# Weight slabs of the QKV and gate projections by casting GpSimd DMAs into one buffer, and other prefetches moved, in an attention and feed-forward layer on eight cores

## The chip, the cores and the metric

The kernel runs on all 8 cores of one Trainium2 chip. No core talks to another: each computes 2048 of the 16384 tokens, with 1536 tokens of history (the halo) in front of them. The metric is the device time of the slowest core, in microseconds.

## What is computed

```python
x = L0_attn_x                                   # (2, 8192, 1024)
xn = layernorm(x)
x = x + attn(xn) + ffn(xn)

def attn(x):                                    # 16 heads of 64, 44 fixed offsets up to 1536
    xn = scale * x / rms(x)
    q, k, v = split(xn @ w_qkv)
    scores[n, o] = q[n] . k[n - offset[o]] / 8 + pos_bias[o]
    out = softmax(scores) weighted sum of v[n - offset[o]]
    gate = sigmoid(xn @ w_gate + b_gate)
    x = x + (out * gate) @ w_out
    xn2 = rmsnorm(x)
    return x + (silu(xn2 @ w_ffn_gate) * (xn2 @ w_ffn_up)) @ w_ffn_down      # 2816 wide

def ffn(x):                                     # 4096 wide, ternary weights with a scale per row
    h = silu(x @ w1 * s1) * (x @ w2 * s2)
    h = gelu(h @ h1 * sh1); h = gelu(h @ h2 * sh2)
    return h @ w3 * s3
```

All tensors come in as f32; the matrix products are made in bf16 with f32 sums.

## The kernel before

The program is written as one list of instructions per engine. Each instruction waits for counters (`tM` counts matmul groups, `vC` VectorE instructions, `sC` ScalarE instructions, one more counter for each DMA stream). VectorE waits for its own previous instruction each time. `DA` puts a DMA on SyncE's (SP's) queue, `DSC` on ScalarE's, `DW` on GpSimd's (POOL's); only the last kind casts f32 to bf16 on the way. Every queue and engine takes its list strictly in order, so a DMA whose wait isn't fulfilled holds all that stand behind it. `barrier()` makes each engine wait for everything issued so far. Five stages follow one another, with a barrier after each.

- **Stage 0, norms (L263 to L423).** Before it, the mask table is written 16 times 512 KB to `d_grep` by 16 DMAs on SP. Then 7 blocks of 512 tokens. For block b: `p0_load(b)` (L325) loads x twice, as f32 into `s_x32` (L329, ScalarE's queue, 2048 KB) and as bf16 into `s_xb` (L333, POOL, 1024 KB written), each with two buffers. `p0_stats` (L338) squares on VectorE (L342) and sums both on TensorE by a column of ones. `p0_rows` (L358) is a chain of small one-partition instructions on VectorE and ScalarE, ending in three broadcasts by TensorE (L382 to L385). `p0_apply` (L389) is 24 VectorE instructions, which leave the normalised block in `s_xnb` and the scaled one in `s_xa`; then a store of `s_xnb` to `d_xn` (L406, on POOL, behind which the next `s_xb` load stands). The order in loop turn b is: load(b+1), rows(b), stats(b+1), apply(b).
- In turns 0 and 1 there is in addition `p1_slab` (L280), which fetches a weight slab for the K projection: twice, an SP DMA of half a slab in f32 (1024 KB) into the single buffer `s_w832` (L284), and a VectorE cast of it into one of two bf16 buffers `s_w8` (L288).
- **Stage 1, projections (L437 to L532).** Eight slabs of 1024 x 512 weights: two for K (448 matmuls together), two for Q (128 each), two for the gate (128 each), two for V (224 each). All but the K slabs call `p1_slab` at their beginning. Its second SP DMA waits for the first cast, and both casts stand in VectorE's list behind the evacuations of the slab before. K and V are kept on chip, Q and the gate go to DRAM through one buffer `s_evq`, so that there each evacuation waits for the store before it.
- **Stage 2, attention (L556 to L764).** The masks come back by 48 SP DMAs (L559), then 16 query tiles of 128 tokens. `p2_tile_loads` (L596) loads the next tile's q and gate on SP in the first head of a tile; pass A (L607) for that tile needs q one head later. At a tile's end the gated rows are stored (L754, SP).
- **Stage 3, output projection and second norm (L766 to L913).** After the barrier POOL issues 144 small loads of scales (L796 to L802); the first `s_xn2` instruction (L905) waits for all of them. `w_out` comes in two f32 halves on ScalarE's queue into one buffer, each followed by a VectorE cast (L810, L815), ahead of all other VectorE work. The gated rows come back in blocks of 4 tiles into two buffers (L828), each block loaded one ahead.
- **Stages 4 and 5**, the two feed-forward nets (L920 to L1143), take their weights by casting POOL DMAs.

## Time and profile before

| what | value |
|---|---|
| runs of the kernel | 4970.8 and 5433.37 us, median 5202.08 |
| the profiled execution | 4969.86 us |
| span on its slowest core (core 7) | 4968.3 us |
| spans of the eight cores | 4939.0 to 4968.3 us |
| granted TensorE clock, mean, core 7 | 0.847 |
| TensorE busy | 3896.4 us, 78% |
| VectorE busy | 1044.5 us, 21% |
| ScalarE busy | 663.1 us, 13% |
| POOL busy | 284.4 us, 6% |
| largest piece of the chain that ended last | matmuls of L1075 (stage 5), 47% |

The profile shows one execution on its slowest core; times are from the first to the last instruction of that core, and some 1.6 us of the execution lie outside of this span. The profiled execution is as long as the shorter of the two runs, so parts of the span can be set directly against 4970 us, and not against the median.

### The profile page before, as it was taken

Reading aid. Unit: us, or ns where it says so; the run is one execution under the profiler, and the core shown is the slowest. Engines: PE = TensorE matmul, PEld = TensorE weight load, DVE = VectorE, ACT = ScalarE, POOL = GpSimd, SP = SyncE. Lnnn points to the kernel's source line nnn. Section 1 sums busy time; section 2 is a strip of 40 time slices with the busy share of each in tenths; the row PEclk is TensorE's granted clock in tenths of the full one; section 3 lists DMA queues with packets and bytes.
Section 4 is the critical chain, followed back from the end, with each engine's and each line's share of the span. In section 5 each row is a group of like instructions: output and inputs, shape, how many; then the busy total and the mean of one; then the engine's idle time right before and its main releaser. Section 6 shows DMA issues by size and latency. Waiting matters only on the chain.

```text
span 4968.3 us, 53354 instructions; the slowest of 8 cores (4939.0 to 4968.3 us)
## 1 busy us (share of the span) xinstructions
PE 3896.4 (78%) x19714; PEld 1847.9 (37%) x19714; DVE 1044.5 (21%) x2055; ACT 663.1 (13%) x802; POOL 284.4 (6%) x310
## 2 busy tenths in 40 slices
PE   1126657455555456998898999999989899999999
PEld 0002223344444212443343444444434344444444
DVE  1564224454555332031011000000010200000001
ACT  0000010344444201200110000000002000000000
POOL 0000000000000510000010000000001000000000
PEclk8557888555555567999999999999999999999999
DMA  5340221100000223205466565656575656565657
GB/s 132 93 102 26 76 76 31 29 20 19 16 21 15 72 78 75 44 1 123 106 76 90 68 85 68 82 71 82 80 152 73 89 70 83 70 83 68 85 68 144
DMA packets 482017, 353.38 MB, mean 71 GB/s; under 512 B 41555, under 2 KB 438868, under 8 KB 479716
## 3 DMA queue, kind: packets, MB, share of 16 engines
q0 software_dynamic: 396064, 216.62, 33.2%
q1 hardware_dynamic: 77364, 114.46, 7.7%
q10 hardware_dynamic: 8336, 18.87, 1.2%
q8 instruction: 164, 2.69, 0.2%
q14 instruction: 89, 0.73, 0.1%
HBM read 513.43 MB, written 53.54 MB: 114 GB/s over the span
## 4 chain that ended last, share of the span: by engine, by line
PE 68%; DVE 12%; DMA 11%; issue 4%; POOL 2%; ACT 1%; DVEq 1%; SPq 1%; another core or an unknown queue 0%; ACTq 0%; POOLq 0%
PE p L1075 47%; DVE s_at L693 4%; PE p_f L950 3%; PE p_f L1009 3%; PE p_f L974 3%; PE p_B L668 3%; PE p_gm L455 2%; PE p_gm L515 2%; DMA s_xb<-xT 2%; PE p_av L715 1%; DMA s_w<-wqkv 1%; DVE s_b L629 1%; DMA d_gate<-s_evq 1%; DMA s_hs<-h1T 1%; PE p_o L869 1%
## 5 line engine op out<-in xcount | busy, mean ns | idle before, releaser
L1075 PE MATMUL p<-s_hb,s_hs 128*128 128x512 bf16 x6144 | 1335.3, 380 | 51.1 <-DMA s_hs<-w1T 24.4
L1075 PE MATMUL p<-s_ha,s_hs 128*128 128x512 bf16 x5120 | 1111.7, 381 | 45.7 <-DMA s_hs<-h1T 37.3
L1075 PEld LDWEIGHTS p<-s_hb,s_hs 128*128 128x128 bf16 x6144 | 598.1, 98 | 788.3 <-issue 76.7
L1075 PEld LDWEIGHTS p<-s_ha,s_hs 128*128 128x128 bf16 x5120 | 500.9, 98 | 656.6 <-issue 55.9
L1133 DVE SCALAR_TENSOR_TENSOR s_oo<-p,s_s,s_rr 128x1024 f32<-128x1024 f32 x16 | 20.5, 1284 | 2005.5 <-PE p L1075 1920.9
L715 PE MATMUL p_av<-s_V,s_at 128*128 128x65 bf16 x2048 | 193.7, 236 | 279.8 <-DVE s_at L693 277.8
L679 ACT ACTIVATE s_E<-p_B,s_negB 128x512 bf16<-128x512 f32 x512 | 351.7, 687 | 421.1 <-PE p_B L668 336.5
L715 PEld LDWEIGHTS p_av<-s_V,s_at 128*128 128x128 bf16 x2048 | 125.3, 118 | 371.9 <-issue 371.6
L668 PE MATMUL p_B<-s_qt,s_K 64*128 64x128 bf16 x2048 | 254.1, 308 | 0.0
L693 DVE TENSOR_TENSOR s_at<-s_E,s_MT 128x512 bf16<-128x512 bf16 x512 | 217.8, 425 | 171.6 <-DVE s_at L693 59.2
L668 PEld LDWEIGHTS p_B<-s_qt,s_K 64*128 64x128 bf16 x2048 | 197.7, 138 | 28.6
L455 PE MATMUL p_gm<-s_xa,s_w 128*128 128x512 bf16 x704 | 158.5, 389 | 53.2 <-DVE s_w L288 27.3
L382 PE MATMUL p_b<-s_row,s_onesf 1*128 1x512 f32 x14 | 14.3, 1122 | 225.2 <-DVE s_row L380 225.2
L1113 ACT ACTIVATE s_ha<-p,s_sh 128x1024 bf16<-128x1024 f32 x64 | 71.2, 1113 | 815.8 <-PE p L1075 815.8
L1113 ACT ACTIVATE s_hb<-p,s_sh 128x1024 bf16<-128x1024 f32 x64 | 71.3, 1113 | 784.9 <-PE p L1075 784.8
L950 PE MATMUL p_f<-s_xn,s_wga 128*128 128x512 bf16 x704 | 154.7, 384 | 20.3 <-DMA s_wga<-wfg 20.3
L1102 DVE SCALAR_TENSOR_TENSOR s_ha<-p,s_s,s_ha 128x1024 bf16<-128x1024 f32 x64 | 82.2, 1284 | 414.7 <-PE p L1075 414.7
L1009 PE MATMUL p_f<-s_hatt,s_wd 128*128 128x512 bf16 x704 | 153.6, 382 | 17.3 <-DMA s_wd<-wfd 17.3
L974 PE MATMUL p_f<-s_xn,s_wga 128*128 128x512 bf16 x704 | 152.1, 379 | 2.2 <-ACT s_hatt L959 2.2
L1096 ACT ACTIVATE s_ha<-p,s_s 128x1024 bf16<-128x1024 f32 x64 | 71.3, 1113 | 502.0 <-PE p L1075 502.0
L515 PE MATMUL p_gm<-s_w,s_xa 128*128 128x512 bf16 x448 | 102.4, 393 | 28.8 <-DVE s_w L288 28.6
L455 PEld LDWEIGHTS p_gm<-s_xa,s_w 128*128 128x128 bf16 x704 | 69.8, 100 | 143.0 <-issue 65.7
(108 smaller groups left out, 1758.8 us busy)
## 6 DMA issues: line engine op xcount, KB each, us to landing
s_hs<-h1T POOLq DMA_DIRECT2D x32, 2048.0 KB, 18.4
s_hs<-h2T POOLq DMA_DIRECT2D x32, 2048.0 KB, 16.1
s_hs<-w1T POOLq DMA_DIRECT2D x32, 512.0 KB, 5.9
s_hs<-w2T POOLq DMA_DIRECT2D x32, 512.0 KB, 5.9
s_hs<-w3T POOLq DMA_DIRECT2D x8, 2048.0 KB, 18.6
s_x<-xT ACTq DMA_DIRECT2D x7, 2048.0 KB, 17.9
s_w<-wqkv SPq DMA_DIRECT2D x12, 1024.0 KB, 5.2
d_grep<-d_gtab SPq DMA_DIRECT2D x16, 512.0 KB, 44.5
```

Source lines behind the costliest of these rows:

```text
L455: T(lambda t, oc4=oc4, kc=kc, b0=b0, b=b, p=p, w83=w83: t.matmul(p[:, b * 512:(b + 1) * 512], w83[:, kc, oc4 * 128:(oc4 + 1) * 128], xa3[: ...
L515: T(lambda t, tt=tt, kc=kc, p=p, w83=w83: t.matmul(p[:, 0:512], xa3[:, kc, tt * 128:(tt + 1) * 128], w83[:, kc, :], start=(kc == 0), stop= ...
L668: T(lambda t, jj=jj, ktile=ktile, g=g, r0=r0, pB=pB, q3=q3: t.matmul(pB[:, jj * 128:(jj + 1) * 128], K3[r0:r0 + 64, g, ktile * 128:(ktile ...
L679: SE(lambda s, pB=pB, par=par, hx=hx, bi=bi: s.activation(s_E[par][:, hx * HW2:(hx + 1) * HW2], pB[:, hx * HW2:(hx + 1) * HW2], AF.Exp, bi ...
L693: V(lambda v, h=h, par=par, hx=hx: v.tensor_tensor(s_at[par][:, hx * HW2:(hx + 1) * HW2], s_E[par][:, hx * HW2:(hx + 1) * HW2], MT3[:, h, ...
L715: T(lambda t, jj=jj, ktile=ktile, h=h, pav=pav: t.matmul(pav[:, 0:65], s_at[par][:, jj * 128:(jj + 1) * 128], V4[:, ktile, h, :], start=(j ...
L950: T(lambda t, oc=oc, kc=kc, b=b, pf=pf: t.matmul(pf[:, b * 512:(b + 1) * 512], wga3[:, kc, oc * 128:(oc + 1) * 128], xn23[:, kc, b * 512:( ...
L974: T(lambda t, oc=oc, kc=kc, b=b, pf=pf: t.matmul(pf[:, b * 512:(b + 1) * 512], wga3[:, kc, oc * 128:(oc + 1) * 128], xn23[:, kc, b * 512:( ...
L1009: T(lambda t, oc=oc, kc=kc, b=b, pf=pf: t.matmul(pf[:, b * 512:(b + 1) * 512], wd3[:, kc, oc * 128:(oc + 1) * 128], ha3[:, kc, b * 512:(b ...
L1075: T(lambda t, o2=o2, kc=kc, b=b, pp=pp, src3=src3, sl3=sl3, n_kc=n_kc: t.matmul(pp[:, b * 512:(b + 1) * 512], sl3[:, kc, o2 * 128:(o2 + 1) ...
L1102: V(lambda v, oc=oc, pp=pp: v.scalar_tensor_tensor(h53[:, oc, :], pp[:, :], s_s2[:, oc:oc + 1], h53[:, oc, :], ALU.mult, ALU.mult), waits= ...
L1113: SE(lambda s, oc=oc, pp=pp: s.activation(dst3[:, oc, :], pp[:, :], AF.Gelu, scale=ssc[:, oc:oc + 1]), waits=[(tM, fm)])
```

## The change

- Stage 0: the f32 load of x and the store to `d_xn` both go to SP's queue. POOL has only the `s_xb` loads left. The two K slabs aren't fetched here any more.
- Stage 1: there is one bf16 slab buffer. Each of the eight slabs is fetched whole by one casting POOL DMA (1024 KB written, 2048 KB read), which waits for the last matmul of the slab before. No cast on VectorE is left.
- Stage 2: the first half of `w_out` comes by a casting POOL DMA at the stage's beginning, and the first block of gated rows by an SP DMA at the end of query tile 3.
- Stage 3: only the second half of `w_out` is fetched in f32 and cast. The gated rows have one buffer, and the load for blocks 1 to 3 waits for the last matmul of the block before.

```diff
-    def p1_slab(src_slab):
-        si = p1w["idx"] & 1
-        p1w["idx"] += 1
-        for hf in range(2):
-            DA(qWS, lambda s, src_slab=src_slab, hf=hf: s.dma_start(
-                w8323[:, :, :], src_slab[:, hf * 4:(hf + 1) * 4, :]),
-               waits=[(vC, p1w["cast_prev"])])
-            wq = qWS.n
-            V(lambda v, si=si, hf=hf: v.tensor_copy(
-                s_w8[si][:, hf * 2048:(hf + 1) * 2048], s_w832[:, :]),
-              waits=[(qWS, wq)] + ([(tM, p1w["mms_done"][si])] if hf == 0 else []))
-            p1w["cast_prev"] = vC.n
-        return si, vC.n
...
-        DSC(qX0[p], lambda s, cslice=cslice, p=p: s.dma_start(
+        DA(qX0[p], lambda s, cslice=cslice, p=p: s.dma_start(
             s_x32[p][:, :].rearrange("p (c t) -> p c t", c=8), xTv[:, :, cslice]),
...
-        DW(qXN[p], lambda s, cslice=cslice, p=p: s.dma_start(
+        DA(qXN[p], lambda s, cslice=cslice, p=p: s.dma_start(
             xn_w[:, :, cslice], s_xnb[p][:, :].rearrange("p (c t) -> p c t", c=8)),
            waits=[(vC, apl_ms)])
...
-        if blk <= 1:
-            k_pre.append(p1_slab(wqkv_v[:, :, D + blk * 512: D + (blk + 1) * 512]))
...
-            if not is_q:
-                si, cast_v = k_pre[wh]
-            else:
-                si, cast_v = p1_slab(wqkv_v[:, :, base_col + wh * 512: base_col + (wh + 1) * 512])
-            w83 = w83v[si]
+            DW(wSL, lambda g, base_col=base_col, wh=wh: g.dma_start(
+                w83[:, :, :], wqkv_v[:, :, base_col + wh * 512: base_col + (wh + 1) * 512]),
+               waits=[(tM, tM.n)])
+            wslabq = wSL.n
...
-        si, cast_v = p1_slab(wgate_v[:, :, wh * 512:(wh + 1) * 512])
-        w83 = w83v[si]
+        DW(wSL, lambda g, wh=wh: g.dma_start(
+            w83[:, :, :], wgate_v[:, :, wh * 512:(wh + 1) * 512]),
+           waits=[(tM, tM.n)])
...
+    DW(qWO, lambda g: g.dma_start(
+        wo3a[:, :, :], wout.ap().rearrange("(k p) o -> p k o", p=128)[:, 0:4, :]))
+    p3_pre = {"g4q0": 0, "woq": qWO.n}
     p2_tile_loads(0)
...
+        if qt == 3:
+            DA(qG4, lambda s: s.dma_start(
+                g43[:, :, :], d_gated.ap().rearrange("n p d -> p n d")[:, 0:4, :]),
+               waits=[(qGD[0], st_p2["gd_store"][0]), (qGD[1], st_p2["gd_store"][1])])
...
-    for wh in range(2):
-        DSC(qWOB, lambda s, wh=wh: s.dma_start(
...
+    DSC(qWOB, lambda s: s.dma_start(
+        s_wo_b32[:, :].rearrange("p (k o) -> p k o", k=4),
+        wout.ap().rearrange("(k p) o -> p k o", p=128)[:, 4:8, :]),
+        waits=[(tM, tM.n)])
+    wob_q = qWOB.n
+    V(lambda v: v.tensor_copy(s_wo_b[:, :], s_wo_b32[:, :]), waits=[(qWOB, wob_q)])
...
-    g4_load(0, [(tM, tM.n), (vC, p2_end_v)])
-    g4_load(1, [(tM, tM.n), (qG4, qG4.n)])
     for blk in range(4):
-        if blk >= 1 and blk + 1 < 4:
-            g4_load(blk + 1, [(tM, tr_ms[blk - 1]), (qG4, qG4.n)])
+        if blk == 0:
+            g4q = p3_pre["g4q0"]
+        else:
+            DA(qG4, lambda s, blk=blk: s.dma_start(
+                g43[:, :, :],
+                d_gated.ap().rearrange("n p d -> p n d")[:, blk * 4:(blk + 1) * 4, :]),
+               waits=[(tM, tM.n)])
```

POOL's list from the first load of stage 0 on, before (L333 is the `s_xb` load, L406 the store of the normalised block):

```order
L333 DMA s_xb<-xT 128x8x512 [waits sC,qG]
L333 DMA s_xb<-xT 128x8x512
L406 DMA d_xn<-s_xnb 128x8x512 [waits vC]
L333 DMA s_xb<-xT 128x8x512 [waits vC,tM]
L406 DMA d_xn<-s_xnb 128x8x512 [waits vC]
L333 DMA s_xb<-xT 128x8x512 [waits vC,tM]
```

The same list in the changed kernel, up to the beginning of stage 2 (L302 is the `s_xb` load; L425, L461 and L491 are the slabs of K and Q, gate, V; L719 is the first half of `w_out`):

```order
L302 DMA s_xb<-xT 128x8x512 [waits sC,qG]
L302 DMA s_xb<-xT 128x8x512
L302 DMA s_xb<-xT 128x8x512 [waits vC,tM] x5
L425 DMA s_w<-wqkv 128x8x512 [waits tM,vC,sC,qC,qG,qX00,qX01,wXB0,wXB1,qXN0,qXN1]
L425 DMA s_w<-wqkv 128x8x512 [waits tM] x3
L461 DMA s_w<-wgate 128x8x512 [waits tM] x2
L491 DMA s_w<-wqkv 128x8x512 [waits tM] x2
L719 DMA s_wo_a<-wout 128x4x1024 [waits tM,vC,sC,qC,qG,qX00,qX01,wXB0,wXB1,qXN0,qXN1,wSL,qES]
```

No store stands between the `s_xb` loads any more, and the eight slab loads stand behind them, the first of them behind the barrier.

SP's list from the mask table on, before (L284 are the half slabs of `p1_slab`):

```order
L259 DMA d_grep<-d_gtab 128x2048 [waits qG] x16
L284 DMA s_w<-wqkv 128x4x512
L284 DMA s_w<-wqkv 128x4x512 [waits vC] x3
L284 DMA s_w<-wqkv 128x4x512 [waits tM,vC,sC,qC,qG,qWS,qX00,qX01,wXB0,wXB1,qXN0,qXN1]
L284 DMA s_w<-wqkv 128x4x512 [waits vC]
L467 DMA d_q<-s_evq 128x1024 [waits vC] x8
```

The same place in the changed kernel (L298 is the f32 load of x, L375 the store of the normalised block):

```order
L259 DMA d_grep<-d_gtab 128x2048 [waits qG] x16
L298 DMA s_x<-xT 128x8x512 [waits sC,qG]
L298 DMA s_x<-xT 128x8x512
L375 DMA d_xn<-s_xnb 128x8x512 [waits vC]
L298 DMA s_x<-xT 128x8x512 [waits vC]
L375 DMA d_xn<-s_xnb 128x8x512 [waits vC]
```

The first two f32 loads of x now stand behind all 16 DMAs of the mask table, and the slabs are gone from this queue.

SP's list in the changed kernel at the end of query tile 3 (L742 stores the gated rows, L746 loads the first block of them, L582 and L587 are the tile loads):

```order
L742 DMA d_gated<-s_gd 128x1024 [waits vC]
L746 DMA s_g<-d_gated 128x4x1024 [waits qGD0,qGD1]
L582 DMA s_qt<-d_q 128x8x128 [waits tM]
L587 DMA s_gtt<-d_gate 128x1024 [waits vC]
L626 DMA_TRANSPOSE s_nbTp<-s_nbp 128x128 [waits vC]
```

The row of L746 is new; the q load of tile 5 (L582) now stands behind a wait for a store and behind a load of 1024 KB.

## Rows read from the trace of the kernel before

**Rows 1.** Windows: PE, PEld, DVE, ACT, POOL busy, PEclk, DMA share, GB/s

```profile
25.60:114.60 89.00, 13.91 (x28) 4.31 (x29) 13.41 (x14) 2.79 (x4) 1.89 (x2) 0.83 0.79 176
114.60:251.80 137.20, 26.93 (x55) 8.26 (x53) 77.99 (x100) 5.58 (x8) 4.36 (x4) 0.54 0.32 85
419.00:851.00 432.00, 324.18 (x1408) 138.46 (x1407) 149.31 (x260) 21.43 (x33) 0.00 (x0) 0.89 0.15 49
```

**Rows 2.** Timeline of stage 0: start, duration, instruction, idle time before it

```profile
112.05 2.29 DVE L342 TENSOR_TENSOR s_xnb<-s_xb 128x4096 bf16<-128x4096 bf16 x1 [18.15 <-DMA s_xb<-xT]
114.58 0.69 DVE L396 TENSOR_TENSOR s_x<-s_x,p_b 128x512 f32<-128x512 f32 x1 [0.24 <-DVE s_xnb L342]
...
134.55 1.23 DVE L288 CAST s_w<-s_w 128x2048 bf16<-128x2048 f32 x1 [0.17 <-DVE s_xa L401]
...
155.69 0.68 DVE L360 COPY s_row<-p_s1b 1x512 f32<-1x512 f32 x1 [0.24 <-DVE s_w L288]
...
193.61 1.23 DVE L288 CAST s_w<-s_w 128x2048 bf16<-128x2048 f32 x1 [0.17 <-DVE s_xa L401]
...
213.92 0.68 DVE L360 COPY s_row<-p_s1a 1x512 f32<-1x512 f32 x1 [0.60 <-DVE s_w L288]
```

**Rows 3.** Timeline of turns 3 and 6 of stage 0, end of rows to apply

```profile
264.39 0.68 DVE L380 TENSOR_TENSOR s_row<-s_row 1x512 f32<-1x512 f32 x1 [1.43 <-ACT s_row L377]
...
270.45 2.29 DVE L342 TENSOR_TENSOR s_xnb<-s_xb 128x4096 bf16<-128x4096 bf16 x1 [5.38 <-DMA s_xb<-xT]
...
272.99 0.69 DVE L396 TENSOR_TENSOR s_x<-s_x,p_b 128x512 f32<-128x512 f32 x1 [0.24 <-DVE s_xnb L342]
...
386.64 0.68 DVE L380 TENSOR_TENSOR s_row<-s_row 1x512 f32<-1x512 f32 x1 [1.12 <-ACT s_row L377]
...
393.20 0.69 DVE L396 TENSOR_TENSOR s_x<-s_x,p_b 128x512 f32<-128x512 f32 x1 [5.88 <-PE p_b L385]
```

**Rows 4.** Waits of stage 1: us in total, times, longest

```profile
PE p_gm L486 <- DVE s_w L288: 35.6, 2, 18.1
PE p_gm L515 <- DVE s_w L288: 28.6, 2, 19.0
PE p_gm L455 <- DVE s_w L288: 27.3, 2, 18.5
```

**Rows 5.** The chain that ended last, at the barrier between stages 0 and 1

```profile
413.48 5.08 DMA d_xn<-s_xnb
418.56 0.35 issue
```

**Rows 6.** DMA issues: queue, KB written by one, median us from issue to landing

```profile
s_hs<-w1T POOLq DMA_DIRECT2D x32, 512.0 KB, 5.9
s_xb<-xT POOLq DMA_DIRECT2D x7, 1024.0 KB, 20.5
s_g<-d_gated SPq DMA_DIRECT2D x4, 1024.0 KB, 10.8
s_xnb<-d_xn SPq DMA_DIRECT2D x4, 1024.0 KB, 5.1
s_wga<-wfg POOLq DMA_DIRECT2D x2, 1280.0 KB, 10.7
```

**Rows 7.** Timeline of TensorE: the last V slab, and a stretch of stage 5

```profile
798.16 51.25 PE L515 MATMUL p_gm<-s_w,s_xa 128*128 128x512 bf16 x224 [9.59 <-DVE s_w L288]
...
2455.99 34.69 PE L1075 MATMUL p<-s_hb,s_hs 128*128 128x512 bf16 x160 [2.02 <-DMA s_hs<-w1T]
```

**Rows 8.** Waits of stage 2

```profile
PE p_A L619 <- DMA s_qt<-d_q: 6.0, 12, 1.2
```

**Rows 9.** Waits of stage 3

```profile
DVE s_wo L815 <- DMA s_wo<-wout: 27.3, 2, 15.5
DVE s_xn L905 <- DMA s_sh<-sh2v: 21.5, 1, 21.5
```

**Rows 10.** Timeline of stage 3 at its third block

```profile
1816.12 6.71 DVE L905 SCALAR_TENSOR_TENSOR s_xn<-s_r,s_g,p_bc 128x512 bf16<-128x512 f32 x8 [3.97 <-PE p_bc L901]
```

More of the change, by code:

```diff
@@ L451, in build_nc @@
                     p = pg[pi]
-                    fw = [(vC, pg_free[pi])] + ([(vC, cast_v)] if (oc4 == 0 and b0 == grps[0][0]) else [])
+                    fw = [(vC, pg_free[pi])] + ([(wSL, wslabq)] if (oc4 == 0 and b0 == grps[0][0]) else [])
                     for kc in range(8):
                         for b in range(gn):
-                            T(lambda t, oc4=oc4, kc=kc, b0=b0, b=b, p=p, w83=w83: t.matmul(
+                            T(lambda t, oc4=oc4, kc=kc, b0=b0, b=b, p=p: t.matmul(
                                 p[:, b * 512:(b + 1) * 512],
@@ L505, in build_nc @@
                waits=[(sC, sv)])
-        p1w["mms_done"][si] = tM.n
     for wh in range(2):
-        si, cast_v = p1_slab(wqkv_v[:, :, 2 * D + wh * 512: 2 * D + (wh + 1) * 512])
-        w83 = w83v[si]
+        DW(wSL, lambda g, wh=wh: g.dma_start(
+            w83[:, :, :], wqkv_v[:, :, 2 * D + wh * 512: 2 * D + (wh + 1) * 512]),
+           waits=[(tM, tM.n)])
+        wvq = wSL.n
         for tt in range(NT):
             p = pg[pi]
-            fw = [(vC, pg_free[pi])] + ([(vC, cast_v)] if tt == 0 else [])
+            fw = [(vC, pg_free[pi])] + ([(wSL, wvq)] if tt == 0 else [])
             for kc in range(8):
-                T(lambda t, tt=tt, kc=kc, p=p, w83=w83: t.matmul(
+                T(lambda t, tt=tt, kc=kc, p=p: t.matmul(
                     p[:, 0:512],
@@ L803, in build_nc @@
     qc2_q = qC2.n
+    woq = p3_pre["woq"]
     qWOB = DS("qWOB")
-    p2_end_t = tM.n
-    p2_end_v = vC.n
-    p2_end_s = sC.n
-    wo_half_v = []
-    for wh in range(2):
-        DSC(qWOB, lambda s, wh=wh: s.dma_start(
-            s_wo32[:, :].rearrange("p (k o) -> p k o", k=4),
-            wout.ap().rearrange("(k p) o -> p k o", p=128)[:, wh * 4:(wh + 1) * 4, :]),
-            waits=[(tM, p2_end_t)] if wh == 0 else [(vC, vC.n)])
-        wob_q = qWOB.n
-        V(lambda v, wh=wh: v.tensor_copy(
-            s_wo[:, wh * 4096:(wh + 1) * 4096], s_wo32[:, :]),
-          waits=[(qWOB, wob_q)])
-        wo_half_v.append(vC.n)
+    DSC(qWOB, lambda s: s.dma_start(
[4 more added lines that the diff above has]
+    V(lambda v: v.tensor_copy(s_wo_b[:, :], s_wo_b32[:, :]), waits=[(qWOB, wob_q)])
+    wob_v = vC.n
     pt_free = [0, 0]
@@ L851, in build_nc @@
                     fw += [(vC, p2_end_v), (sC, p2_end_s)]
-                T(lambda t, ttl=ttl, c=c, pt=pt, g43=g43: t.transpose(
+                T(lambda t, ttl=ttl, c=c, pt=pt: t.transpose(
                     pt[:, :], g43[:, ttl, c * 128:(c + 1) * 128], s_id[:, :]),
@@ L861, in build_nc @@
         gT_ms = vC.n
-        tr_ms[blk] = tM.n
         for oc in range(8):
             po = p_o3[oc & 1]
-            fw = [(vC, max(po_free[oc & 1], gT_ms))] + \
-                 ([(vC, wo_half_v[0])] if (blk == 0 and oc == 0) else [])
-            fw4 = [(vC, wo_half_v[1])] if (blk == 0 and oc == 0) else ()
+            fw = [(vC, max(po_free[oc & 1], gT_ms))] + ([(qWO, woq)] if (blk == 0 and oc == 0) else [])
+            fw4 = [(vC, wob_v)] if (blk == 0 and oc == 0) else ()
             for kc in range(8):
-                T(lambda t, kc=kc, po=po, oc=oc: t.matmul(
-                    po[:, :], wo3[:, kc, oc * 128:(oc + 1) * 128], gT3[:, kc, :],
+                wv = wo3a[:, kc, oc * 128:(oc + 1) * 128] if kc < 4 else                      wo3b[:, kc - 4, oc * 128:(oc + 1) * 128]
+                T(lambda t, kc=kc, po=po, wv=wv: t.matmul(
+                    po[:, :], wv, gT3[:, kc, :],
                     start=(kc == 0), stop=(kc == 7)),
@@ L914, in build_nc @@
         st3.close()
+        st3pre.close()
         ctx.close()
@@ L1025, in build_nc @@
     st3.close()
+    st3pre.close()
     if upto == 4:
```

63 lines of the change are left out of this document (28 added, 35 removed).

## The prediction

> **What bounds the kernel now.** I read the windows view first, cut at the barriers. Stages 4 and 5, of which L1075 alone is 47% of the chain in the table above, keep TensorE busy and aren't touched. In what the change touches, no engine is full: in the first 89 us after the x loads are issued VectorE is busy for 13 us, and the 16 DMA engines for 0.79 of the time, moving 176 GB/s; then for 137 us VectorE is busy for 78 and the DMA engines for 0.32 [rows 1]. So stage 0 is bound by DMA at first, and then by a chain through VectorE with holes in it. In stage 1 TensorE works 324 of 432 us [rows 1]. The timeline and the waits show where the holes are: at slabs of weights [rows 2, 4].
>
> **Stage 0, the K slabs.** In turns 0 and 1 VectorE runs into a cast whose second half needs an SP DMA that is issued only after the first cast. From the first cast to the next useful instruction it takes 155.69 - 134.55 = 21.1 us in turn 0 and 213.92 - 193.61 = 20.3 us in turn 1 [rows 2]. Nothing else runs on VectorE meanwhile, and the rows chain that follows was ready. Both stalls go: **-41.2 us** (0.2 us of an ordinary step stay). What could be late next is x of the following block. The f32 load of block 1 would be needed at about 145 instead of 174, and it is the last of SP's first batch, at some 120 by the sum below.
>
> **Stage 0, xb loads.** Before, the s_xb load of block b+1 stands on POOL behind the store of block b-1, which waits for the apply. In an undisturbed turn the apply begins 393.20 - 386.64 = 6.56 us after the last row instruction begins; in turn 3, where s_xb is late, it takes 272.99 - 264.39 = 8.60 us, so 2.0 are lost [rows 3]. Turns 3, 4 and 5 have this pattern: **-6 us**. The store now stands on SP; it was never what the next block waited for, and the x32 load behind it has a whole turn of time.
>
> **Stage 0, the front.** This price the trace doesn't show. Before, three queues shared the DMA engines: 8.4 MB of mask table on SP, 4.2 MB of x32 on ScalarE's queue, 2.1 MB of s_xb written (4.2 read) on POOL, and 1 MB of K slab. All was done when s_xb of block 1 came, at 112, and the first apply began at 114.6 [rows 2]. Now x32 of block 0 stands behind the whole table. Ahead of its landing are 8.4 + 2.1 MB on SP and 2.1 to 3.1 MB on POOL (the third s_xb load may now start as soon as block 0's sums are made). At 176 GB/s [rows 1] that is 72 to 77 us, landing at 98 to 103. Counted by bytes read, the old batch was 17.9 MB in 89 us, 201 GB/s, and what is ahead now is 16.8 MB, 84 us: landing at 109. I take the middle, 106, against 114.6: **-8 us**, with +5 and -16 as ends (x32 held up by all of POOL's traffic; everything at the better rate and s_xb early).
>
> The Trainium skill ("DMA: Bandwidth & Descriptors", section Queues, rings and completion order) says that each DMA engine takes turns between the queues that have work, packet by packet. With two queues instead of three POOL's share grows, which brings s_xb earlier; that agrees with the first s_xb load being late beside two other queues. It doesn't say how much x32 loses by it, and the sum doesn't use it.
>
> **Stage 1.** TensorE's holes at the six slabs for Q, gate and V are 27.3 + 35.6 + 28.6 = 91.5 us [rows 4]: two half loads with two casts, made one after the other, and in Q and the gate also the rest of the evacuation chain, since the casts stand behind it. Afterwards a hole is from the last matmul to the landing of one casting POOL load, since the stores of the old slab are done by then. A load of this very shape is s_xb, median 20.5 us [rows 6], but always beside 2 to 3 MB of other traffic. Alone stand the w1T loads, 512 KB in 5.9 us, and the wfg loads, 1280 KB in 10.7 [rows 6]; on the line between them 1024 KB take 9.1. A hop over a semaphore costs 0.35 [rows 5]. So a hole is **9.5 us**, with 6.3 and 21 as ends.
> - Six holes of 9.5 instead of 91.5: 57.0 - 91.5 = -34.5 us.
> - The first K slab, loaded by stage 0 before, comes after the barrier: +9.1 us.
> - The second K slab: K ran through 448 matmuls without a hole. Now there is one of 9.5, and the matmuls after it begin at the low clock: after the hole of 9.59 us, 224 matmuls took 51.25 us, where at the rate of stage 5 (34.69 / 160 = 0.217) they take 48.6 [rows 7]. So +9.5 + 2.7 = +12.2 us.
>
> Together **-13.2 us**. The same clock loss stood behind the old holes, so it isn't counted again for them.
>
> The Trainium skill (the same page, section Anatomy of one DMA, SWDGE path) gives a POOL DMA 2.0 us plus its bytes at 436 GB/s. An estimate from that page: 6.8 us for the 2 MB that are read, a hole of 7.2, and a sum for stage 1 near -32 instead of -13. The trace speaks against it, as w1T takes 5.9 where the page gives 4.4 for its 1 MB of reads.
>
> **Stage 2.** At the end of tile 3 SP waits for the store of the gated rows (2 us, nearest row 5.1 for a whole MB store [rows 5]) and issues a load of 1 MB, before the q load of tile 5. That q load has no slack: pass A already waits for it, 6.0 us over 12 tiles [rows 8]. A plain SP load of 1 MB takes 5.1 us [rows 6]. So one wait of about 2 + 5, less what goes in parallel: **+6 us**, ends 0 and 11. The wout load on POOL meets the 48 mask loads on SP: **+1 us**, ends 0 and 9 (its own time alone, 9.1, if it went wholly ahead).
>
> **Stage 3.** Half of the wait for wout goes, up to 15.5 us of the 27.3 [rows 9]. But the first s_xn instruction still stood idle for 21.5 us, until the last of 144 small POOL loads had landed [rows 9], and these begin at the same barrier as before. Whatever is early before it only makes that wait longer: **0**, ends -3 and +3 for the spacing of those loads. The single buffer for gated rows: the load of blocks 2 and 3 starts when the broadcast is done, and beside it VectorE has 6.7 us of s_xn work [rows 10] before it can take the first transpose. A load of 5.1 [rows 6] is hidden; at the median of 10.8 that these loads had in mixed traffic [rows 6] two of them would cost 8. I take **0**.
>
> **Sum.** -41.2 - 6 - 8 - 13.2 + 6 + 1 + 0 = -61.4 us. Against the profiled execution of 4969.9 us that is **4908.5 us**. The median of the two runs, 5202, is the mean of 4970.8 and 5433; I forecast for executions like the shorter.
>
> **Rivals.**
> 1. *The slab loads are as slow as s_xb.* Eight cores read the same slab at once, and the only row of this shape says 20.5 us [rows 6]. A hole is 21: 11.4 us more for each of eight, +91, in all 4999.7 us, slower than before. Against it: w1T and wfg are also read by eight cores at once. It decides from a hole of 9.5 + 61.4 / 8 = 17.2 us on. Chance 0.06.
> 2. *The front loses.* x32 of block 0 behind 8.4 MB of table comes at 120, not 106: +14 us, 4922 us. For it: the table's DMAs are the first on the queue, and POOL's loads take their share of the engines beside them. Against it: the byte sum. Chance 0.2.
> 3. *All the open prices come out low.* Hole of 6.3 us as for w1T (-26), front at 98 (-8), stage 2 for nothing (-7): 4868 us. For it: nothing else is on the DMA engines at the slabs, their share in stage 1 is 0.15 [rows 1]. Chance 0.12.
> 4. *The stalls don't go but move.* Without the 21 us pauses the x loads of turns 1 and 2 could be late, so half of the 41 comes back: 4929 us. For it: in turn 3 s_xb was late already [rows 3]. Against it: that load now starts a turn earlier. Chance 0.08.
>
> The forecast itself holds 0.54. A measurement of this kernel can tell about 2% (99 us) from no change. Rival 3 ends just past that bound and half of its weight lies beyond; rival 1's upper part alone and anything unforeseen reach past 5069. So: faster by over 2% 0.08, within 2% 0.88, slower 0.04. The range from 4868 to 4960 holds the forecast's own spread (each end: the front 8, the holes about 20, stage 2 5, and for the upper end rival 4), and leaves out rival 1 and the lower half of rival 3.
>
> **What would show it.** In the changed profile: no VectorE idle of 17 us in turns 0 and 1; turns 3 to 5 shorter by 2 us each; the first apply near 106; eight TensorE holes of 9 to 10 us each, two of them in K; one wait of pass A for s_qt of some 6 us in the fifth tile; the first s_xn still waiting for s_sh and ending as long after the barrier as before; stages 4 and 5 unchanged within 5 us. The prediction is wrong if the holes are over 17 us, if the first apply is later than 120, or if the stage after the first barrier keeps a wait that I didn't name.

## The result, and the profile after

| | before | after |
|---|---|---|
| runs | 10, median 5009.15 us (4960.42 to 5433.37) | 11, median 4908.27 us (4904.18 to 5533.5) |
| profiled execution | 4969.86 us | 4904.18 us |
| span of the slowest core | 4968.3 us (core 7) | 4902.6 us (core 4) |

The ratio after to before is 0.9842 with a 95% interval from 0.9804 to 0.988: the change is a gain, and a small one, within 2%. The two profiled executions, which the stretches below compare, give 4904.18 / 4969.86 = 0.987. The forecast was 4908.5 us, a ratio of 0.988 to the profiled execution. Several executions of either kernel are 2 to 13% longer on some cores whatever the kernel does, and the comparisons leave these out, but not three executions of the kernel before at 5006.65 to 5013.75 us, without which the ratio would be 0.988 too.

One execution of one core wanders by 10 us and more where nothing was changed. So I cut the span at landmarks (the start of the first or last instruction of a line), on each of the eight cores, and took the median over the cores. Each column is a stretch in us:

| kernel | start to first apply | to first K matmul | to end of V (last evacuation) | to first pass A matmul | to last exponential | to first `s_xn` | first to last `s_xn` | rest |
|---|---|---|---|---|---|---|---|---|
| before | 113.2 | 303.4 | 431.3 | 30.1 | 788.4 | 98.1 | 157.8 | 3030.9 |
| after | 111.9 | 264.1 | 408.9 | 32.0 | 795.8 | 91.9 | 158.2 | 3032.0 |
| difference | -1.3 | -39.3 | -22.4 | +1.9 | +7.4 | -6.2 | +0.4 | +1.1 |
| forecast | -8 | -38.1 | -22.3 | +1 | +6 | 0 | 0 | 0 |

(The second column is the difference of the medians of two landmarks. The forecast there is -41.2 - 6 + 9.1, the last for the first K slab; that of the third column is -34.5 + 12.2.) The differences add up to -58.4 us; the median of the eight spans fell from 4955.8 to 4892.8, by 63.0, and the slowest core's by 65.7. Differences of medians need not add up exactly, and in one execution the rest alone is 3018 to 3045 us from core to core.

Stage 0 after: windows of core 4 (PE, PEld, DVE, ACT, POOL busy, PEclk, DMA share, GB/s), which answer to [rows 1].

```profile
25.00:112.00 87.00, 16.41 (x38) 5.13 (x38) 13.40 (x13) 2.79 (x4) 3.63 (x4) 0.84 0.97 162
112.00:375.00 263.00, 60.74 (x116) 19.23 (x116) 183.10 (x239) 16.74 (x24) 3.49 (x4) 0.55 0.41 93
```

Until the first apply the DMA engines are now busy for 0.97 of the time (0.79 before) and move less, 162 GB/s for 176. All eight cores show it: 0.90 to 0.97 with 161 to 167 GB/s after, 0.78 to 0.89 with 176 to 177 before. VectorE's timeline on core 4 (start, duration, instruction, idle time before it and what ended it) has the first blocks; it answers to [rows 2, 3].

```profile
67.01 2.29 DVE L311 TENSOR_TENSOR s_xnb<-s_xb 128x4096 bf16<-128x4096 bf16 x1 [52.00 <-DMA s_xb<-xT]
97.59 2.29 DVE L311 TENSOR_TENSOR s_xnb<-s_xb 128x4096 bf16<-128x4096 bf16 x1 [12.47 <-DMA s_xb<-xT]
112.61 0.69 DVE L365 TENSOR_TENSOR s_x<-s_x,p_b 128x512 f32<-128x512 f32 x1 [12.73 <-DMA s_x<-xT]
...
145.38 2.29 DVE L311 TENSOR_TENSOR s_xnb<-s_xb 128x4096 bf16<-128x4096 bf16 x1 [0.24 <-DVE s_row L349]
151.02 0.69 DVE L365 TENSOR_TENSOR s_x<-s_x,p_b 128x512 f32<-128x512 f32 x1 [3.35 <-PE p_b L354]
```

The square of block 1 came early, at 97.59 and not at 112.05, and then VectorE had to wait for x in f32 until 112.61. From there on the turns are clean: the square follows the last row instruction after 0.24 us and no slab stall is left. A turn takes 38 us (112.61 to 151.02 is the first).

Stage 1 after: TensorE's timeline on core 4. Of the eight rows before which it stood idle for a slab these are the first of each kind and the last, and they answer to [rows 7].

```profile
378.03 50.16 PE L437 MATMUL p_gm<-s_xa,s_w 128*128 128x512 bf16 x224 [36.58 <-DMA s_w<-wqkv]
438.47 50.65 PE L437 MATMUL p_gm<-s_xa,s_w 128*128 128x512 bf16 x224 [10.29 <-DMA s_w<-wqkv]
...
581.91 9.32 PE L469 MATMUL p_gm<-s_w,s_xa 128*128 128x512 bf16 x32 [11.18 <-DMA s_w<-wgate]
...
738.92 50.89 PE L499 MATMUL p_gm<-s_w,s_xa 128*128 128x512 bf16 x224 [10.16 <-DMA s_w<-wqkv]
```

The same holes as waits of stage 1 (us in total, times, longest), answering to [rows 4], and then the chain that ended last at the first and second slab (start, us, what), answering to [rows 5].

```profile
PE p_gm L437 <- DMA s_w<-wqkv: 68.0, 4, 36.6
PE p_gm L469 <- DMA s_w<-wgate: 20.9, 2, 11.2
PE p_gm L499 <- DMA s_w<-wqkv: 19.6, 2, 10.2
PE p_gm L469 <- DVE s_gt L477: 14.3, 23, 1.1
```

```profile
361.06 4.98 DMA d_xn<-s_xnb
...
366.21 0.49 issue
366.69 11.20 DMA s_w<-wqkv
...
428.24 0.49 issue
428.73 9.61 DMA s_w<-wqkv
438.34 0.14 issue
```

On core 4, the slowest, the seven holes behind the first add up to 68.0 - 36.6 + 20.9 + 19.6 = 71.9 us, 10.3 each; one such hole is a load of 9.61 plus 0.49 and 0.14 of issue. It is the core with the longest holes: the same sum is 65.4 to 71.9 us over the eight cores, median 66.8, which is 9.5 each. DMA issues (queue, KB written by one, median us to landing), answering to [rows 6]:

```profile
s_w<-wqkv POOLq DMA_DIRECT2D x6, 1024.0 KB, 9.6
s_xb<-xT POOLq DMA_DIRECT2D x7, 1024.0 KB, 20.9
s_g<-d_gated SPq DMA_DIRECT2D x4, 1024.0 KB, 5.6
```

The slab load and the `s_xb` load have the same shape and differ in these medians by a factor of two. What makes the difference is the traffic beside them: the three `s_xb` loads that fly alone (issued at 157.6, 195.3 and 233.1 us, landed at 168.0, 206.0 and 243.0, core 4) took 10.4, 10.7 and 9.9 us, as long as a slab, and the four of the crowded first 125 us took 20.9 to 71.1. Last, the waits in the middle of stage 2 and in stage 3 (core 4), which answer to [rows 8, 9].

```profile
PE p_A L603 <- DMA s_qt<-d_q: 10.7, 12, 6.8
...
DVE s_xn L883 <- DMA s_sh<-sh2v: 34.3, 1, 34.3
DVE s_wo_b L802 <- DMA s_wo_b<-wout: 11.1, 1, 11.1
PE p_t L831 <- DMA s_g<-d_gated: 17.6, 3, 5.9
```

Pass A now has one wait of 6.8 us for a q tile, where its longest was 1.2. The first `s_xn` still waits for the chain of small loads, and longer (34.3 us for 21.5), since everything before it is earlier.

### The profile page after: what moved, and what is told of

The parts are those of the page before. It is cut to its first block, busy times and chain, and to the rows that moved or that the text cites. A ratio compares the mean times of both kernels' runs of the same rounds, so it can differ in the third digit from the quotient of the medians.

```text
span 4902.6 us, 53299 instructions; the slowest of 8 cores (4875.9 to 4902.6 us)
## 1 busy us (share of the span) xinstructions
PE 3890.3 (79%) x19714; PEld 1851.6 (38%) x19714; DVE 1021.5 (21%) x2038; ACT 663.1 (14%) x802; POOL 282.9 (6%) x312
## 4 chain that ended last, share of the span: by engine, by line
PE 71%; DVE 12%; DMA 7%; issue 4%; ACT 2%; POOL 2%; DVEq 1%; SPq 1%; another core or an unknown queue 1%; ACTq 0%; POOLq 0%
PE p L1055 49%; DVE s_at L677 4%; PE p_gm L437 3%; PE p_f L988 3%; PE p_f L929 3%; PE p_f L953 3%; PE p_B L652 3%; PE p_gm L499 2%; PE p_av L699 1%; DMA s_w<-wqkv 1%; DMA s_hs<-h1T 1%; DVE s_b L613 1%; PE p_o L847 1%; DVEq L58 1%; DVE s_xa L370 1%
## 5 line engine op out<-in xcount | busy, mean ns | idle before, releaser
L1055 PEld LDWEIGHTS p<-s_ha,s_hs 128*128 128x128 bf16 x5120 | 501.4, 98 | 650.4 <-issue 49.1
L1113 DVE SCALAR_TENSOR_TENSOR s_oo<-p,s_s,s_rr 128x1024 f32<-128x1024 f32 x16 | 20.5, 1284 | 1999.9 <-PE p L1055 1898.7
L351 PE MATMUL p_b<-s_row,s_onesf 1*128 1x512 f32 x14 | 14.3, 1122 | 190.4 <-DVE s_row L349 190.4
L499 PE MATMUL p_gm<-s_w,s_xa 128*128 128x512 bf16 x448 | 101.0, 389 | 19.7 <-DMA s_w<-wqkv 19.6
```

The costliest lines, as they stand in the source:

```text
L499: T(lambda t, tt=tt, kc=kc, p=p: t.matmul(p[:, 0:512], xa3[:, kc, tt * 128:(tt + 1) * 128], w83[:, kc, :], start=(kc == 0), stop=(kc == 7) ...
L1055: T(lambda t, o2=o2, kc=kc, b=b, pp=pp, src3=src3, sl3=sl3, n_kc=n_kc: t.matmul(pp[:, b * 512:(b + 1) * 512], sl3[:, kc, o2 * 128:(o2 + 1) ...
```

## Experiments

Stretches without another source are the medians over the eight cores of one profiled execution, as in the table above. Where no ratio is given, one to three executions were made, and the reading rests on the stretches and not on the time.

**1. The front: x on ScalarE's queue again, in the changed kernel.**

```diff
-        DA(qX0[p], lambda s, cslice=cslice, p=p: s.dma_start(
+        DSC(qX0[p], lambda s, cslice=cslice, p=p: s.dma_start(
```

> The changed kernel, with only the f32 load of x back on ScalarE's queue. In the changed kernel VectorE waited 12.7 us for s_x in turn 0 and the first apply began at 112.3 us, though s_xb of block 1 was there at 97.6. Theory (x32 of block 0 is held by its place behind the 8.4 MB mask table on SP): now VectorE waits for s_xb again and the first apply begins between 96 and 106, the end of stage 0 comes 6 to 15 us earlier, all else stays. Rival (the DMA engines carry a fixed batch and what comes last sets the time, whatever the queue): the first apply begins at 108 to 114 again, since s_xb now comes later by what x32 gains. Total: theory 4893 to 4901, rival 4905.

The profiled execution's slowest core took 4908.2 us (4902.6 in the changed kernel), and the median of the eight spans is 4893.0 (4892.8): the same. The first apply began at 112.2 (111.9). VectorE's timeline on core 4:

```profile
109.98 2.29 DVE L311 TENSOR_TENSOR s_xnb<-s_xb 128x4096 bf16<-128x4096 bf16 x1 [17.94 <-DMA s_xb<-xT]
112.51 0.69 DVE L365 TENSOR_TENSOR s_x<-s_x,p_b 128x512 f32<-128x512 f32 x1 [0.24 <-DVE s_xnb L311]
```

The wait changed its name and not its end. On SP x comes last and `s_xb` early; on ScalarE's queue it is the other way round. Both are needed for the apply, so the queue doesn't matter here. The rival stated above holds.

**2. The front again: the third `s_xb` load held back.** In the changed kernel:

```diff
-           waits=[(vC, p0["sq_v"][p]), (tM, p0["stat_tm"][p])] + gw)
+           waits=[(vC, p0["apl_v"][0] if blk == 2 else p0["sq_v"][p]), (tM, p0["stat_tm"][p])] + gw)
```

> The changed kernel with one load held back: the s_xb load of block 2 waits for the apply of block 0 again, as it did in effect in the kernel before. In the changed kernel the first apply waits 12.7 us for x in f32 and begins at 112.3. Theory: what lands last in the first batch is set by the bytes on the DMA engines, and the third s_xb load puts 2.1 MB written (4.2 MB read) among them; without it the first apply begins near 106, as I had forecast. The wait in the second or third turn for s_xb comes back in exchange (2 us). Rival: x in f32 stands behind the table on SP and is bound by that queue alone; then the first apply stays at 112.

The first apply began at 104.1 (median; 102.2 on core 4, 106.1 on core 7) instead of 111.9. Core 4's timeline:

```profile
102.17 0.69 DVE L365 TENSOR_TENSOR s_x<-s_x,p_b 128x512 f32<-128x512 f32 x1 [5.79 <-DMA s_x<-xT]
...
142.62 2.29 DVE L311 TENSOR_TENSOR s_xnb<-s_xb 128x4096 bf16<-128x4096 bf16 x1 [7.54 <-DMA s_xb<-xT]
```

So it was the third load, issued as soon as the sums of block 0 were made (at 73.0 us on core 4 of the changed kernel, landed at 112.3, x at 112.5), that put 8 us before the first apply. Held back, it is late for its own block by 7.5 us; of the 7.8 gained, 3.8 were left at the first K matmul (372.2 for 376.0), and nothing in the slowest core's span (4901.9).

**3. The store of the normalised block on SP, alone.** In the kernel before:

```diff
-        DW(qXN[p], lambda s, cslice=cslice, p=p: s.dma_start(
+        DA(qXN[p], lambda s, cslice=cslice, p=p: s.dma_start(
```

> The kernel before, with only the store of the normalised block moved from POOL's queue to SP's. Theory (s_xb was late in turns 3 to 5 because its load stood behind the store, which waits for the apply): VectorE's idle time before the square in these turns, 5.4 to 6.3 us, falls to 0.24, each turn is 2 to 3 us shorter, first K matmul 6 to 8 us earlier (at 411 to 413); the two stalls of 20 us at the K slabs stay. Rival (s_xb is late because it shares the DMA engines with x32): turns 3 to 5 stay at 41 us.

The first K matmul came at 413.3 (416.6 before), only 3 us sooner, and 1.9 of that lie before the first apply (111.3 for 113.2). The time, 4972.54 us, isn't told from the kernel before. The `s_xb` waits of turns 3 to 5 went as forecast (0.24 us of idle before each of these squares). But in turns 0 and 1, VectorE's timeline on core 7, the slab stalls grew (here turn 0; turn 1 has 16.32 and 5.63):

```profile
148.11 1.23 DVE L288 CAST s_w<-s_w 128x2048 bf16<-128x2048 f32 x1 [16.51 <-DMA s_w<-wqkv]
155.60 1.23 DVE L288 CAST s_w<-s_w 128x2048 bf16<-128x2048 f32 x1 [6.26 <-DMA s_w<-wqkv]
```

Before, the first of the two casts didn't wait, and 21 us were lost in all; now it is 16.5 + 6.3 and the instructions themselves, some 25. The half slab stands behind a store on SP now. The two parts of the change are no independent sum: the store's move pays only where the slabs have left stage 0.

**4. The slabs out of stage 0, alone.** In the kernel before:

```diff
-        if blk <= 1:
-            k_pre.append(p1_slab(wqkv_v[:, :, D + blk * 512: D + (blk + 1) * 512]))
...
-            if not is_q:
-                si, cast_v = k_pre[wh]
-            else:
-                si, cast_v = p1_slab(wqkv_v[:, :, base_col + wh * 512: base_col + (wh + 1) * 512])
+            si, cast_v = p1_slab(wqkv_v[:, :, base_col + wh * 512: base_col + (wh + 1) * 512])
```

> The kernel before, with only the two K slabs taken out of stage 0 and fetched at their place in stage 1 by the same routine (two f32 halves on SP, two casts on VectorE). Theory: stage 0 loses both stalls, 41 us less 2 us for each of turns 1 and 2, where s_xb now comes late as in turns 3 to 5: first K matmul at 418.9 - 37 + 13 (two half loads of 5.1 and two casts of 1.2 behind the barrier) = 395; the second K slab makes a hole of 9 us in K and 2.7 us of slow matmuls behind it; in all -12 us against the kernel before, ratio 0.9976. Rival (the stalls only move, x loads become late in their place): first K matmul at 418 or later, in all +12 us or more, ratio 1.002 or above.

Ratio to before 0.9966, 95% from 0.995 to 0.9982. The first K matmul came at 394.8 (416.6), with a first slab of two half loads in that time already; stage 1 became longer, 442.7 (431.3). The stalls are gone, but VectorE's timeline on core 7 has a wait for `s_xb` in each of five turns, of which the first is:

```profile
150.06 2.29 DVE L342 TENSOR_TENSOR s_xnb<-s_xb 128x4096 bf16<-128x4096 bf16 x1 [5.88 <-DMA s_xb<-xT]
```

This is the fourth rival (stalls that move) in a small form: without the 21 us pauses the loads behind the store on POOL are late in turns 1 and 2 too. In the changed kernel the store is gone from POOL, and the waits with it.

**5. The early load of gated rows taken out of stage 2.** In the changed kernel (block 0 is then loaded in stage 3 like the others):

```diff
-        if qt == 3:
-            DA(qG4, lambda s: s.dma_start(
-                g43[:, :, :], d_gated.ap().rearrange("n p d -> p n d")[:, 0:4, :]),
-               waits=[(qGD[0], st_p2["gd_store"][0]), (qGD[1], st_p2["gd_store"][1])])
```

> The changed kernel, with the load of the first block of gated rows taken out of query tile 3 and made at the beginning of stage 3. Theory (this load stands in front of the q load of tile 5 on SP's queue): the wait of pass A for s_qt of 6.8 us goes, the waits for s_qt fall from 10.7 to 4 to 6 us in total, stage 2 is 5 to 7 us shorter, and stage 3 doesn't get longer, because its first block waits for the 144 small POOL loads anyway: that wait shrinks from 34 to no less than 25 us. Total -6 us. Rival (the load was hidden in stage 2 and its absence costs in stage 3): stage 2 as long as before, stage 3 5 to 10 us longer.

First pass A matmul to last exponential: 790.8 us instead of 795.8, in line with the wait for `s_qt` (core 4):

```profile
PE p_A L603 <- DMA s_qt<-d_q: 5.0, 12, 1.0
```

It fell from 10.7 to 5.0. From the last exponential to the first `s_xn` it took 92.4 (91.9). So the early load costs 5 us and buys 0.6. The time, 4907.03, isn't told from the changed kernel's.

**6. The first half of `w_out` at the end of query tile 1.** In the changed kernel:

```diff
-    DW(qWO, lambda g: g.dma_start(
-        wo3a[:, :, :], wout.ap().rearrange("(k p) o -> p k o", p=128)[:, 0:4, :]))
...
+        if qt == 1:
+            DW(qWO, lambda g: g.dma_start(
+                wo3a[:, :, :], wout.ap().rearrange("(k p) o -> p k o", p=128)[:, 0:4, :]),
+               waits=[(vC, gd_ms)])
```

> The changed kernel with the load of the first half of w_out moved from the beginning of stage 2 to the end of query tile 1, when no engine waits for a DMA. Before the change the first pass A matmul began 29.7 and 30.1 us (cores 7 and 4) after the end of V, in the changed kernel 32.1 and 33.8. Theory: the half of w_out takes its share of the engines beside the mask loads and makes the first q and mask tiles late; then it falls back to 30, and the wait elsewhere in stage 2 does not grow. Rival: the 2 to 4 us belong to the barrier and to stores of stage 1 that end later, and stay.

End of V to the first pass A matmul: 29.9 us, as before the change (30.1), instead of 32.0. Beside the mask loads the half of `w_out` costs 2 us. Behind it pass A to the last exponential took 796.9 (795.8), and the time isn't told from the changed kernel's (lowest 4911.76).

**7. The casts of `w_out` on ScalarE.** In the kernel before (the waits for these casts then count ScalarE's instructions):

```diff
-        V(lambda v, wh=wh: v.tensor_copy(
-            s_wo[:, wh * 4096:(wh + 1) * 4096], s_wo32[:, :]),
+        SE(lambda s, wh=wh: s.activation(
+            s_wo[:, wh * 4096:(wh + 1) * 4096], s_wo32[:, :], AF.Copy),
```

> The kernel before with the two casts of w_out made by ScalarE and not by VectorE; nothing else. In the kernel before two issues of small loads on POOL take 2.46 us each, where the others take 0.54, and these two begin with VectorE's two casts of w_out (2.29 us each) to 0.05 us. Theory: a cast of VectorE from f32 to bf16 holds up POOL's issue of a DMA. Then both issues fall back to 0.54 us, and the chain of 144 loads, from the barrier to the first s_xn 98 us, becomes about 4 us shorter. Rival: the long issues come from the transfers beside them (the load of the second half of w_out), and stay where the loads are.

In the kernel before (core 7) the rows of POOL and VectorE in question are:

```profile
1686.69 2.46 POOL L799 DMA_DIRECT2D s_s<-s1v  x1
1686.74 2.29 DVE L815 CAST s_wo<-s_wo 128x4096 bf16<-128x4096 f32 x1 [15.51 <-DMA s_wo<-wout]
...
1700.73 2.46 POOL L802 DMA_DIRECT2D s_sh<-sh2v  x1
1700.78 2.29 DVE L815 CAST s_wo<-s_wo 128x4096 bf16<-128x4096 f32 x1 [11.75 <-DMA s_wo<-wout]
...
1733.75 2.59 POOL L801 DMA_DIRECT2D s_sh<-sh1v  x1
1733.92 2.29 DVE L885 CAST s_r1b<-s_r 128x4096 bf16<-128x4096 f32 x1
...
1747.32 0.54 POOL L800 DMA_DIRECT2D s_s<-s2v  x1 [7.83 <-issue]
```

With the casts on ScalarE (core 7) one long issue is left, beside the one cast that VectorE still makes:

```profile
1685.76 3.62 ACT L815 ACTIVATE s_wo<-s_wo 128x4096 bf16<-128x4096 f32 x1 [19.37 <-DMA s_wo<-wout]
...
1722.97 2.44 POOL L799 DMA_DIRECT2D s_s<-s1v  x1
1722.99 2.29 DVE L885 CAST s_r1b<-s_r 128x4096 bf16<-128x4096 f32 x1
...
1738.80 0.54 POOL L800 DMA_DIRECT2D s_s<-s2v  x1 [4.92 <-issue]
```

The last exponential to the first `s_xn` fell from 98.1 to 91.5 us, as far as by the whole change (91.9). Of the 6.6 us, 2 x 1.92 are the two issues, and 7.83 - 4.92 = 2.9 a gap of POOL whose cause I didn't find. The two long issues fell to 0.54, as the theory had it. The lowest time was 4957.06 us, beside 4967.27 for the kernel before.

**8. The 144 small loads at the start of stage 2.** In the changed kernel the block of code from `qC2 = DS("qC2")` to `qc2_q = qC2.n` stands ahead of `p2_tile_loads(0)`, behind the load of `w_out`, and not behind the barrier of stage 3:

```diff
+    qC2 = DS("qC2")
+    for c in range(8):
+        DW(qC2, lambda s, c=c: s.dma_start(s_g2[:, c:c + 1], g2v.ap()[c * 128:(c + 1) * 128].unsqueeze(1)))
...
     p2_tile_loads(0)
```

> The changed kernel with the 144 small loads of scales and shifts issued on POOL at the start of stage 2, behind the load of the first half of w_out, and not at the barrier before stage 3. Theory: at the start of stage 3 nothing but this chain of small loads holds the first s_xn instruction; in the changed kernel it waits 34 us for s_sh and comes 92 us after the last exponential. Without the chain it comes some 30 us earlier, bound by the output projection of the first block and the statistics, and since stage 3 runs on from there, the kernel takes about 4875 us where the changed kernel takes 4905 (ratio to the kernel before near 0.979). Rival: the 34 us are hidden by TensorE's own backlog in stage 3, so that the first s_xn comes early and the last s_xn at the same time; then the time stays within 5 us of the changed kernel's. Second rival: 144 small loads beside the mask loads of stage 2 delay pass A by as much as they give back.

Ratio to before 0.9827, 95% from 0.9798 to 0.9855, against 0.9842 for the changed kernel, which was set against other executions of the kernel before; the lowest times, 4883.56 us and 4904.18, and the cores' spans show the difference better. The last exponential to the first `s_xn` took 60.8 us instead of 91.9, and the gain lasts to the last `s_xn` (159.0 us for 158.2). So the first rival, TensorE's backlog, is out. The row of the first `s_xn` (core 4) has no DMA before it any more:

```profile
1674.46 6.70 DVE L883 SCALAR_TENSOR_TENSOR s_xn<-s_r,s_g,p_bc 128x512 bf16<-128x512 f32 x8 [3.88 <-PE p_bc L879]
```

The second rival has a part: the first pass A matmul came 36.5 us after the end of V (32.0), and pass A to the last exponential took 797.6 (795.8). Of 31 us 6 are given back there, and the median of the spans fell by 24.7 (4868.1).

**9. Two slab buffers.** In the changed kernel, a load is issued into the other buffer as soon as the slab before last is used up; there is no early load of gated rows:

```diff
+    def slab_load(i):
+        if i < 8:
+            DW(wSL[i & 1], lambda g, i=i: g.dma_start(w83v[i & 1][:, :, :], slabs[i]),
+               waits=[(tM, sl_end[i - 2])] if i >= 2 else ())
+            slq[i] = wSL[i & 1].n
...
+            sl_end[cur] = tM.n
+            slab_load(cur + 2)
```

> The changed kernel with two buffers for the slabs of stage 1, each slab's load issued as soon as the slab before the one in use has been used up, and without the early load of gated rows (which makes room in SBUF). Theory: a hole of TensorE in stage 1 is the whole duration of one slab load and nothing else, 9.4 to 11 us each after the first; seven of them go, 70 us, and with them the low clock behind each, some 2 us. So stage 1 (first K matmul to the last evacuation of V, 415 us in the changed kernel) becomes 335 to 345 us, stage 2 is 5 us shorter as without the early gated rows, and the kernel takes about 4830 us. Rival: TensorE at this granted clock is limited by power, and without the pauses the granted clock of stage 1 falls, so that less than half comes back: 4865 us or more. The first slab's hole of 36 us stays in both.

Ratio 0.9756, 95% from 0.9734 to 0.9779; lowest run 4850.02 us. Stage 1 took 355.4 us instead of 408.9, 53.5 less and not the 70 to 80 expected. TensorE's timeline on core 7, and then the window of the stage (columns as in [rows 1]):

```profile
378.54 110.21 PE L451 MATMUL p_gm<-s_xa,s_w 128*128 128x512 bf16 x496 [36.87 <-DMA s_w<-wqkv]
...
571.19 1.89 PE L485 MATMUL p_gm<-s_w,s_xa 128*128 128x512 bf16 x8 [0.69 <-DVE s_gt L493]
...
639.38 95.57 PE L517 MATMUL p_gm<-s_w,s_xa 128*128 128x512 bf16 x440 [0.51 <-DVE s_gt L493]
```

```profile
378.00:738.00 360.00, 320.73 (x1408) 137.35 (x1408) 134.72 (x249) 21.42 (x33) 5.31 (x7) 0.97 0.20 44
```

Its waits for the evacuations, and the window of the same stage in the changed kernel (core 4):

```profile
PE p_gm L485 <- DVE s_gt L493: 24.5, 23, 5.3
PE p_gm L451 <- DVE s_evq L460: 7.9, 5, 3.6
...
378.00:788.00 410.00, 323.61 (x1401) 138.35 (x1402) 132.56 (x242) 21.42 (x33) 6.11 (x7) 0.90 0.18 39
```

No slab hole is left. The 0.7 us before each of the gate's groups of 8 were there before (14.3 us in all, core 4); what is new are waits for evacuations of up to 3.6 us in Q and up to 5.3 in the gate. On the median of the eight cores these waits grew from some 15 to some 35 us, so of the 66.8 us of holes about 46 are left as a gain. The remaining 7 of the 53.5 are probably matmuls that no longer begin again behind a hole; nothing here separates them. That is the step that my expectation left out. The rival fell clearly: the granted clock rose to 0.97, from 0.90 in the changed kernel and 0.89 in the one before [rows 1].

**10. All three parts together** (two slab buffers and no early gated rows, the small loads at the start of stage 2, x on ScalarE's queue): the diffs of experiments 9, 8 and 1.

> The changed kernel with two slab buffers and no early gated rows, with the small loads at the start of stage 2, and with x in f32 on ScalarE's queue again. The theory has the parts apart from each other: 4905 less 75 (slabs and gated rows) less 30 (small loads) less 0 to 2 (first apply bound by the DMA engines either way) is about 4800 us, a ratio to the kernel before near 0.963. Rival: the early small loads stand behind the two slab buffers' last loads or beside the masks and cost stage 2 some 10 us, 4815 us or more.

Ratio 0.9709, 95% from 0.9687 to 0.9731; median 4829.93 us, lowest 4824.95. The stretches: stage 1 355.3, end of V to pass A 37.1, stage 2 792.4, to the first `s_xn` 64.0. By the median of the eight spans experiment 8 gave 24.7 us and experiment 9 gave 58.3, and together they give 74.2, 9 less than the sum. Some 3 us of this are at the first `s_xn` (64.0 for 60.8), and 5.5 in the stretch behind the last `s_xn` (3033.0 for 3027.5 in experiment 9), which nobody changed. By the lowest times nothing is missing: 4904.18 less 20.62 and 54.16 is 4829.4. So the 4800 that I expected failed by what experiments 8 and 9 had each fallen short, and the rival's 4815 or more is what came. It is faster than both kernels.

**11. The same with the half of `w_out` and the small loads at the end of query tile 1**, by a wait for the tile's last VectorE instruction as in experiment 6.

> The kernel with two slab buffers, no early gated rows, x in f32 on ScalarE's queue and the small loads in stage 2, but with the half of w_out and the 144 small loads issued at the end of query tile 1 and not at the stage's beginning. In the version with them at the beginning, the first pass A matmul came 35.8 to 38.7 us after the end of V (30 in the kernel before), and stage 2 took 792.2 to 793.0 us where it takes 789.8 without the small loads. Theory: at the end of tile 1 they meet nothing that is waited for, and 8 to 10 us of both come back: about 4815 us. Rival: 144 small DMAs cost pass A the same wherever they stand, and the time is 4825 again.

Ratio 0.973, 95% from 0.9711 to 0.9749, median 4835.53, lowest 4826.77 us. End of V to pass A took 30.4 us for 37.1, so there 6.7 us come back as expected; pass A to the last exponential stayed at 792.8, 2.9 above the 789.9 of experiment 9, so there the small loads cost the same wherever they stand, and of the rival that half held. The time isn't told from experiment 10's, and the two intervals overlap. That the 6.7 us don't show in it stays open; they are 0.14%.

## Why the prediction was right, and where not

**The K slabs and the `s_xb` waits, -41.2 and -6, with +9.1 for the first slab: right.** First apply to first K matmul fell by 39.3 us, forecast 38.1. It is right in its parts too: up to the last apply it fell from 297.5 to 248.4 us (-49.1, forecast -47.2), and from there to the first K matmul it grew from 6.0 to 15.5 (+9.5, forecast +9.1). The two terms were argued one by one, and experiments 3 and 4 show that each alone would have given less: the store alone 3 us, since the slab stalls grow, and the slabs alone left waits of 6 us, 2 of which are lost each time, in five turns. The forecast held because the change does both.

**The front, -8: wrong in size.** It was -1.3 us (111.9 for 113.2). The step that failed is the sum of bytes ahead of x, in its amount and in its rate. I allowed POOL "2.1 to 3.1 MB" there. The third `s_xb` load, possible as soon as the sums of block 0 are made, came in whole among them; without it the first apply is at 104.1 (experiment 2), which is 2 us better than the 106 forecast. And I took 176 GB/s from the kernel before, while the engines moved 161 to 167 here. The end that counted bytes read, with all three `s_xb` loads, gave 109 and came nearest; taking the middle between it and the other was a guess. That `s_xb` would be earlier was right, by 15 us (97.59 for 112.05), and worth nothing, since x was then last and the apply needs both (experiment 1). The rival of 120 us didn't occur.

**Stage 1, -13.2, or -22.3 from the first K matmul on: right**, -22.4 us. So was the hole: 9.5 us over the eight cores, forecast 9.5. The line drawn through w1T and wfg gave a load of 9.1, where the median of the six wqkv loads is 8.2 to 9.6 by core, and the hop over semaphores was 0.63 us instead of 0.35; the two differences are small and of opposite sign. Core 4 alone, with 10.3, would say that seven holes cost 5 us more than forecast. (Behind the 10.29 us hole, 224 matmuls took 50.65 us, 2.0 more than at the rate of 0.217, where I had counted 2.7 once.) The first rival, loads as slow as `s_xb`'s 20.5 us, is out by the same rows: what makes those slow is what flies beside them, and the three that fly alone take 9.9 to 10.7.

An estimate from the Trainium skill ("DMA: Bandwidth & Descriptors", Anatomy of one DMA, SWDGE path) stood beside the sum with 6.8 us for this load. It took 8.2 to 9.8 by core (medians of the wqkv and the wgate loads). The measurement decides; why the page's rate isn't reached no run here shows.

**Stage 2, +6 and +1: right in place, a bit small.** The early gated rows cost 5.0 (experiment 5), the half of `w_out` 2.1 (experiment 6). The stage is 9.3 us longer and not 7; 2.4 us between pass A and the last exponential (790.8 for 788.4) stay unexplained.

**Stage 3, 0: wrong by 6.2 us.** I wrote that the wait for the small loads "only" becomes longer, since they begin at the same barrier. The length of their chain isn't fixed, though. The 144 issues took 89.7 to 91.7 us from core to core before, and 83.0 to 85.4 after. About 1.9 of this is the cast of `w_out` that VectorE no longer makes: experiment 7, with both casts taken away, shows that each holds up one issue by 1.9 us. The larger part is the one gap of POOL within the chain, 7.8 to 9.9 us before and 3.3 to 5.5 after. It was shorter in experiment 7 too, 3.8 to 6.7, but its cause stays open. TensorE waits for the single buffer of gated rows 5.9 us three times, as long as a load takes, and this costs nothing, as forecast: first to last `s_xn` is 158.2 us for 157.8.

**Stages 4 and 5, 0: right**, +1.1 on the median core. On core 7 alone it looked like -12, which is why a single core's landmarks are no measure for terms of this size.

So that the total hit to within 5 us is in part luck: the front's miss (+6.7) and stage 3's (-6.2) cancel. The two stretches with forecasts of over 10 us came within 1.2 us of them, and that isn't.

## What to carry to other kernels

Where several loads that are needed together share the DMA engines, count all that may start before the last of them lands, also those that a change sets free; here the queue decided only which came last (first apply at 111.9 and 112.2 us). When a stall is removed, look for the load that had been in its shadow: each of two edits here gave back a part of its gain at the other's place. And look for the side on which a buffer's second copy hides a load that nothing else hides: one slab buffer more won 54 us in stage 1, where the room had gone to an early load of gated rows that cost 5 us and won 0.6. Last, when a term is some 10 us, read it on all cores: the slowest one had the longest holes.
